# Result stores split over the batches: 128 KB stores with 32 batches outermost for 256 KB stores with four time quarters outermost

## Chip, cores and metric

One core of a Trainium2 chip runs the whole program. The metric is the device time of one execution in microseconds (us), lower is better. The core has a TensorE, a VectorE, a ScalarE, a GpSimd and a SyncE queue, and 16 DMA engines shared by all transfers.

## What is computed

`x` is 64 batches x 128 channels x 2048 times, fp32. First a mixing of channels by a matrix that each batch chooses, with a residual. Then a long convolution along time per channel (a state-space kernel of 64 complex modes and a direct term `D`), masked by a length per batch, again with a residual.

```
x = x + einsum('bct,bcd->bdt', x, weights[cond])            # mixing
dt = exp(log_dt); A = -exp(log_A_real) + 1j * A_imag; dtA = A * dt[:, None]
Ct = Cc * (exp(dtA) - 1.0) / A
K = 2.0 * einsum('hn,hnl->hl', Ct, exp(dtA[:, :, None] * arange(T))).real
y = causal_convolution(x, K) + x * D[:, None]               # by an FFT of 2T
out = x + y * (arange(T)[None, :] < length[:, None])[:, None, :]
```

## The kernel before

The mixed `x` goes through a scratch in device memory, `u_scratch`, laid out so that one channel and 32 batches are a tile of 128 rows of 512 times: row `t * 32 + b` holds quarter `t` of the time for batch `b` (`NBW` = 32, `UNIT` = 512 elements or 2 KB, `HALF` = 1024). The work after the mixing runs in 64 slots (`NSL`). A slot handles four such tiles, v = 0 to 3. A wide slot takes four channels and one half of the batches, the others two channels and both halves (`channel(s, v)`, `batches(s, v)`). The first 12 slots (`WIDE`) are wide, later every fourth one is. `made` slots compute the tables of their channels anew, the others load tables that were stored.

The engines run a software pipeline over `c`, the slot number, to `NSL + 2`. In turn `c` TensorE transposes the rows of slot c + 1 (`transpose_u`, L774), makes states of slot c (L797, L814) and the outputs of slot c - 1 (L835, L841, L853), in eight steps k. ScalarE empties output banks into `o_sb` (L972), VectorE then lays the unmasked input over it (`overlay`, L1255: where a batch is past its length the input stands in the result) and counts it in `s_ov`. In the first ten turns (`LATER` = 10) TensorE also mixes the last 28 batches (L752), two or three of them in a turn, in between these steps; their stores to `u_scratch` and the loads of `x_f` go with them.

`o_sb` is four buffers of 128 rows x 2 tiles x 512 elements. Buffer `2 * (s % 2) + v // 2` holds tiles 2p and 2p + 1 of slot s. ScalarE waits at L971 until the stores of the slot two before have landed (`s_store`). Nearly all transfers are issued by SyncE, in a fixed order. In a later turn `c` it is: the first half of `u_row` for slot c + 2 (`load_u`, L426), the table transposed by DMA (`transpose_g`, L486) or loaded (L472) for slot c + 1, the stores of tiles 2 and 3 of slot c - 2, the second half of `u_row`, the Toeplitz table (L440), at times a table of `g` (L462), and the stores of tiles 0 and 1 of slot c - 1. `load_u` waits for the overlay that frees its buffer:

```python
b, last = ROW_AT[s], before(ROW_AT, s)
if last is not None:
    sp.wait_ge(s_ov, 4 * last + 2 * p + 2)
```

In the turns with mixing, `mixing_slot`, the store of tile 3 of slot c - 2 is issued in step 0 and those of tiles 0, 1 and 2 of slot c - 1 in steps 3, 5 and 7, among stores to `u_scratch` (`store_half`, L417) and loads of `x_f` (L407). Two of the last slot's stores are issued by ScalarE.

Of the kernel before, what the change touches and what calls it, by code (L numbers as in the profile page):

```python
# [16 lines left out]
NB, H, T = 64, 128, 2048  # L17
# [16 lines left out]
UNIT = 512  # L34
# [9 lines left out]
NBW = NB // 2  # L44
# [3 lines left out]
LATER = len(MIXED)  # L48
# [17 lines left out]
NSL = len(SLOTS)  # L66
# [48 lines left out]
def before(places, i):  # L115

    last = [j for j in range(i) if places[j] == places[i]]
    return last[-1] if last else None
# [27 lines left out]
def build(nc, x, cond, length, w_in, log_dt, c_in, log_a, a_im, d_in, out):  # L146
# [8 lines left out]
    with ctx:  # L155
        def sb(name, shape, dt, where=ctx):
            return where.enter_context(nc.sbuf_tensor(name, shape, dt))

        def sem(name):
            return ctx.enter_context(nc.semaphore(name))  # L160
# [87 lines left out]
        o_sb = [sb(f"o_sb{i}", [P, 2, UNIT], F32, outs) for i in range(4)]  # L248
# [20 lines left out]
        s_store = [sem(f"s_store{i}") for i in range(4)]  # L269
# [9 lines left out]
        s_out, s_y, s_ov = (sem(n) for n in ("s_out", "s_y", "s_ov"))  # L279
# [17 lines left out]
        def has(c):  # L297
            return 0 <= c < NSL

        def wait(eng, s, value):  # L300
            if value > 0:
                eng.wait_ge(s, value)
# [31 lines left out]
        def mixing_over(eng):  # L334
            batch_mixed(eng, NB - 1)
# [11 lines left out]
        def channel(s, v):  # L347
            return SLOTS[s].first + (v if SLOTS[s].wide else v // 2)

        def batches(s, v):  # L350
            return SLOTS[s].part if SLOTS[s].wide else v % 2
# [35 lines left out]
                stored_g(eng, last)  # L387
            return gt_sb[GT_AT[unit.of]][:, unit.part, :, :, :].rearrange("p a b m -> p (a b m)"), half

        def store_out(eng, s, v):  # L390

            o = 2 * (s % 2) + v // 2
            eng.wait_ge(s_ov, 4 * s + v + 1)
            dst = bass.AP(out.tensor, batches(s, v) * NBW * H * T + channel(s, v) * T, [[UNIT, 4], [H * T, NBW], [1, UNIT]])
            eng.dma_start(dst, o_sb[o][:, v % 2, :]).then_inc(s_store[o], 16)  # L395

        @block.sync
        def _(sp):
# [4 lines left out]
            def load_x(n):  # L403
                last = before(X_AT, n)
                if last is not None:
                    batch_mixed(sp, last)
                sp.dma_start(x_f[X_AT[n]][:, :], x[n, :, :]).then_inc(s_x[X_AT[n]], 16)  # L407

            def store_half(n, j):
                if n < FIRST:  # L410
                    sp.wait_ge(s_ev, 2 * n + j + 1)
                else:
                    for q in (2 * j, 2 * j + 1):
                        evacuated(sp, UNIT_OF[Unit(True, n, q)])
                b = STAGE_AT[2 * n + j]
                dst = bass.AP(u_dram, (n // NBW * P + 2 * j * NBW + n % NBW) * UNIT, [[2 * TILE, H], [NBW * UNIT, 2], [1, UNIT]])
                sp.dma_start(dst, stage[b][:, :].rearrange("p (a t) -> p a t", t=UNIT)).then_inc(s_us[b], 16)  # L417

            def load_u(s, p):
# [4 lines that stand above are left out]
                step = (channel(s, 1) - channel(s, 0)) * 2 + batches(s, 1) - batches(s, 0)  # L424
                src = bass.AP(u_dram, (channel(s, 2 * p) * 2 + batches(s, 2 * p)) * TILE, [[UNIT, P], [step * TILE, 2], [1, UNIT]])
                sp.dma_start(u_row[b][:, HALF * p:HALF * (p + 1)].rearrange("p (v t) -> p v t", t=UNIT), src)\  # L426
                    .then_inc(s_row[b][p], 16)

            def load_toeplitz(s):
                t0, n = TABS[s][0], len(TABS[s])  # L430
                together = n == 2 and TOEP_AT[t0] % 4 < 3 and TOEP_AT[t0 + 1] == TOEP_AT[t0] + 1
                for t in [t0] if together else TABS[s]:
                    for r in range(t, t + 1 + together):
                        last = before(TOEP_AT, r)
                        if last is not None:
                            sp.wait_ge(s_out, 4 * (SLOT_OF[last] + 1))
                    b, rows_ = TOEP_AT[t], 4 * (1 + together)
                    src = bass.AP(k_dram, PAIR_OF[t] * (4 * KROW), [[1, P], [KROW, rows_], [1, Q]])
                    to = ap((toep_now, toep_later)[b // 4], b % 4 * 4 * Q, [[Q, rows_], [1, Q]])
                    sp.dma_start(to, src).then_inc(s_t[b], 16)  # L440

            def store_g(s):

                t = TABS[s][0]
                r = t // 2 % (GS // 2)
                sp.wait_ge(s_g, 4 * (MADE_NO[t] + 2))
                dst = bass.AP(g_dram, PAIR_OF[t] * P * 4 * Q, [[4 * Q, P], [P * 4 * Q, 2], [1, 4 * Q]])
                sp.dma_start(dst, ap(g_all, t % GS * 4 * Q, [[4 * Q, 2], [1, 4 * Q]])).then_inc(s_gst[r], 16)
                for unit in turns_of(s):
                    evacuated(sp, UNIT_OF[unit])  # L450
                dst = bass.AP(gt_dram, PAIR_OF[t] * P * 4 * Q, [[4 * Q, P], [P * 4 * Q, 2], [1, 4 * Q]])
                sp.dma_start(dst, ap(gt_now, 0, [[4 * Q, 2], [1, 4 * Q]])).then_inc(s_gtst[r], 16)
# [71 lines left out]
            def mixing_slot(c):  # L524
                for k in range(8):
                    if k == 0:
                        if c > 0:
                            load_toeplitz(c)
                        if has(c - 2):
                            store_out(sp, c - 2, 3)  # L530
                        load_u(c + 1, 1)
                    if k == 1:
                        store_g(c)
                    if k == 3 and c == 0:
                        sp.wait_ge(s_kd, 80)
                        load_toeplitz(c)
                    if k in (3, 5, 7) and has(c - 1):
                        store_out(sp, c - 1, k // 2 - 1)
                    if k == 5:
                        load_u(c + 2, 0)  # L540
                    for u in UNITS_AT[c][k]:
                        n, q = UNITS[u].of, UNITS[u].part
                        if UNITS[u].batch and q % 2 == 1:
                            store_half(n, q // 2)
                        if UNITS[u].batch and q == 3 and n + 3 < NB:
                            load_x(n + 3)

            def slot(c):
                if c < LATER:
                    mixing_slot(c)  # L550
                    return
                if c == LATER:
                    load_toeplitz(c)
                    store_out(sp, c - 2, 3)
                    load_u(c + 1, 1)
                    stages_landed(sp, range(STAGES // 2), NB)
                    mixing_over(sp)
                    load_toeplitz(c + 1)
                if has(c + 2):
                    load_u(c + 2, 0)  # L560
                if c < WIDE:
                    store_g(c)
                if c + 1 >= WIDE and has(c + 1):
                    if SLOTS[c + 1].made:
                        transpose_g(c + 1)
                    else:
                        load_gt(c + 1)
                if has(c - 2) and c > LATER and c - 2 < NSL - 1:
                    for v in (2, 3):
                        store_out(sp, c - 2, v)  # L570
                if has(c + 2):
                    load_u(c + 2, 1)
                    load_toeplitz(c + 2)
                    if not SLOTS[c + 2].made:
                        load_g(c + 2)
                if has(c - 1) and c - 1 < NSL - 1:
                    for v in range(2):
                        store_out(sp, c - 1, v)
                elif has(c - 1):
                    for v in (0, 2):  # L580
                        store_out(sp, c - 1, v)

            slots(slot)
            for o in range(4):
                sp.wait_ge(s_store[o], 32 * (NSL // 2))

        @block.gpsimd
        def _(pool):
# [304 lines left out]
        def _(act):  # L893
# [73 lines left out]
            def out_evac(s, v):  # L967
                o = 2 * (s % 2) + v // 2
                act.wait_ge(s_out, 4 * s + v + 1)
                if v % 2 == 0:  # L970
                    wait(act, s_store[o], 32 * (s // 2))  # L971
                act.activation(o_sb[o][:, v % 2, :], bank[:, 2 + v % 2, :], ACT.Copy, scale=1.0 / (US * KS))\  # L972
                    .then_inc(s_y, 1)

# [29 lines left out]
                                g_hi(t)  # L1004

            slots(slot)
            for v in (1, 3):
                store_out(act, NSL - 1, v)

        @block.vector  # L1010
        def _(dve):
# [302 lines left out]
```

## Time and profile before

| | |
|---|---|
| median of 3 runs | 1378.93 us (1374.29 to 1379.3) |
| profiled execution | 1383.85 us, span 1381.8 us |
| TensorE busy | 1099.5 us (80% of the span) |
| VectorE, ScalarE, GpSimd busy | 763.9, 576.3, 580.1 us |
| granted TensorE clock | 0.915 of full |
| moved by DMA | 330.88 MB, 239 GB/s over the span |
| stores of results | 254 issues on SyncE, 2 on ScalarE, 256 KB each |

In the rows, PE is TensorE and PEld its weight load, DVE VectorE, ACT ScalarE, POOL GpSimd, SPq and ACTq the queues from which SyncE and ScalarE issue transfers. L395 is line 395 of the kernel. PEclk is the granted clock as a share of 2.4 GHz, DMA share the mean busy share of the 16 DMA engines. Packets that overlap a little bring a share slightly over 1.

### The profile page before, as it was taken

What the parts mean: (1) busy time and instruction counts of PE and PEld (TensorE: products, weight loads), DVE (VectorE), ACT (ScalarE), POOL (GpSimd) and SP (SyncE); (2) the same over time, 40 slices, a digit from 0 to 9 for tenths busy, and PEclk for the clock granted to TensorE, in tenths of its full rate; (3) what the DMA queues carried; (4) which work ended last, traced back from release to release, by engine and by line L of the source; (5) the groups of instructions that cost most, each with busy time, mean ns of one, the idle gap of its engine ahead of it and who ended that gap; (6) DMA issues with size and microseconds to landing.
All of it is one profiled execution on the core that took longest, in us unless ns stands there. A gap on an engine that the chain in (4) does not pass through costs nothing.

```text
span 1381.8 us, 33160 instructions
## 1 busy us (share of the span) xinstructions
PE 1099.5 (80%) x12910; PEld 835.4 (60%) x12910; DVE 763.9 (55%) x1754; ACT 576.3 (42%) x1275; POOL 580.1 (42%) x1377
## 2 busy tenths in 40 slices
PE   8787858877877698787888787888778888888783
PEld 4332425555555467676767766767667767676663
DVE  5989314544544346556555565656555565656552
ACT  3544433333443334344444444444444444444431
POOL 2110388433433424453543444444644435444500
PEclk9999979988998889999999999999999998999987
DMA  9999999888988876997979897979988898979782
GB/s 349 408 416 416 415 351 346 305 295 293 314 317 296 282 243 194 177 191 193 184 196 175 193 163 186 190 195 197 167 205 172 203 171 195 193 192 195 161 145 101
DMA packets 218107, 330.88 MB, mean 239 GB/s; under 512 B 53138, under 2 KB 98578, under 8 KB 209762
## 3 DMA queue, kind: packets, MB, share of 16 engines
q1 hardware_dynamic: 217530, 328.05, 86.6%
q8 instruction: 104, 1.70, 0.6%
q0 software_dynamic: 160, 0.20, 0.1%
q10 hardware_dynamic: 264, 0.52, 0.1%
q14 instruction: 49, 0.40, 0.1%
HBM read 171.25 MB, written 147.00 MB: 230 GB/s over the span
## 4 chain that ended last, share of the span: by engine, by line
DMA 48%; PE 34%; SPq 7%; DVE 4%; ACT 3%; issue 3%; POOLq 0%; DVEq 0%; POOL 0%; ACTq 0%
DMA u_row<-u_scratch 36%; DMA u_scratch<-stage 9%; PE bank L835 6%; PE bank L853 6%; PE bank L752 6%; PE bank L774 5%; PE bank L797 4%; SPq L395 3%; PE bank L740 3%; PE bank L841 2%; PE bank L814 2%; SPq L462 2%; DVE o_sb L1255 2%; DVE u_t L1233 1%; ACT u_t L949 1%
## 5 line engine op out<-in xcount | busy, mean ns | idle before, releaser
L774 PE MATMUL bank<-ident,u_row 128*128 128x128 f32 x1024 | 295.6, 292 | 188.4 <-DMA u_row<-u_scratch 183.2
L853 PE MATMUL bank<-g_sb,st_sb 128*128 128x256 f16 x1536 | 330.0, 288 | 2.1 <-issue 2.1
L637 POOL TENSOR_TENSOR g_sb<-g_x,g_sb 128x128 f16<-128x128 f32 x256 | 103.0, 436 | 497.6 <-ACT g_sb L921 497.6
L1233 DVE SCALAR_TENSOR_TENSOR u_t<-bank,u_t 128x512 f16<-128x512 f32 x256 | 176.0, 688 | 192.1 <-ACT u_t L949 191.1
L774 PEld LDWEIGHTS bank<-ident,u_row 128*128 128x128 f32 x1024 | 150.5, 148 | 214.5 <-DMA u_row<-u_scratch 195.5
L965 ACT ACTIVATE st_sb<-bank 128x128 f16<-128x128 f32 x448 | 123.9, 277 | 309.3 <-PE bank L814 214.4
L949 ACT ACTIVATE u_t<-bank 128x512 f16<-128x512 f32 x256 | 151.9, 594 | 192.1 <-PE bank L774 192.1
L1238 DVE TENSOR_TENSOR st_sb<-bank,st_sb 128x128 f16<-128x128 f32 x448 | 130.2, 291 | 171.2 <-ACT st_sb L965 165.5
L835 PE MATMUL bank<-toep,u_t 128*128 128x192 f16 (+1 forms) x1752 | 208.4, 226 | 0.0
L1255 DVE COPY_PREDICATED o_sb<-mask,u_row 128x512 f32<-128x512 uint8 x256 | 194.5, 760 | 17.0 <-issue 16.9
L853 PEld LDWEIGHTS bank<-g_sb,st_sb 128*128 128x128 f16 x1536 | 156.9, 103 | 11.0 <-issue 2.4
L740 PE MATMUL bank<-x_f,w_buf 128*128 128x512 f32 x280 | 133.4, 626 | 36.0 <-issue 23.7
L835 PE MATMUL bank<-toep_later,u_t 128*128 128x192 f16 (+1 forms) x1320 | 156.7, 227 | 2.7 <-issue 2.7
L814 PE MATMUL bank<-st_sb,lam_sb 128*128 128x32 f16 (+1 forms) x3168 | 147.2, 184 | 10.1 <-issue 7.4
L972 ACT ACTIVATE o_sb<-bank 128x512 f32<-128x512 f32 x256 | 152.9, 598 | 4.4 <-DMA out<-o_sb 2.2
L814 PEld LDWEIGHTS bank<-st_sb,lam_sb 128*128 128x128 f16 x3168 | 132.3, 97 | 37.0 <-issue 21.8
L835 PEld LDWEIGHTS bank<-toep,u_t 128*128 128x128 f16 x1752 | 139.7, 103 | 11.0 <-issue 3.5
L629 POOL TENSOR_TENSOR g_x<-g_x,g_y 128x128 f32<-128x128 f32 x256 | 126.1, 523 | 5.0
L752 PE MATMUL bank<-x_f,w_buf 128*128 128x512 f32 x232 | 125.0, 648 | 2.3 <-ACT stage L926 1.9
L644 POOL TENSOR_TENSOR lam_sb<-eyes,lam_v 128x128 f16<-128x128 f16 x256 | 110.2, 459 | 32.3 <-PE bank L814 32.2
L740 PEld LDWEIGHTS bank<-x_f,w_buf 128*128 128x128 f32 x280 | 53.5, 199 | 110.6 <-issue 100.2
L936 ACT ACTIVATE stage<-bank 128x1024 f32<-128x1024 f32 x70 | 70.4, 1022 | 113.6 <-DMA u_scratch<-stage 74.6
(142 smaller groups left out, 1545.0 us busy)
## 6 DMA issues: line engine op xcount, KB each, us to landing
x_f<-in_x SPq DMA_DIRECT2D x64, 1024.0 KB, 14.1
u_scratch<-stage SPq DMA_DIRECT2D x128, 512.0 KB, 12.3
u_row<-u_scratch SPq DMA_DIRECT2D x128, 512.0 KB, 9.6
out<-o_sb SPq DMA_DIRECT2D x254, 256.0 KB
toep<-k_scratch SPq DMA_DIRECT2D x16, 512.0 KB, 10.9
g_scratch<-g_sb SPq DMA_DIRECT2D x12, 512.0 KB, 8.9
gt_scratch<-gt_sb SPq DMA_DIRECT2D x12, 512.0 KB, 8.9
toep_later<-k_scratch SPq DMA_DIRECT2D x24, 256.0 KB, 7.9
```

The costliest lines, as they stand in the source:

```text
L629: pool.tensor_tensor(out=g_x[r][:, h, part], in0=g_x[r][:, h, part], in1=g_y[:, h, part], op=SUB)\
L740: last = pe.matmul(bank[:, 4 * (n % 2) + k, :], w_buf[n % WS][:, :], x_f[X_AT[n]][:, k * 512:(k + 1) * 512], start=True, stop=True)
L752: last = pe.matmul(to, w_buf[of % WS][:, :], x_f[X_AT[of]][:, part * 512:(part + 1) * 512], start=True, stop=True)
L774: ins = pe.transpose(bank[:, u_bank(s, v), k % 4 * P:(k % 4 + 1) * P], ap(u_row[b], v * UNIT + g * Q + tb * P, [[1, P]]), ident[:, :])
L814: last = pe.matmul(ap(bank, v * 2 * P + at(j), [[2 * P, n], [1, NBW]]), lam_sb[t % LS][:, h, a, :, :].rearrange("p k m -> p (k m)"), st_sb ...
L835: pe.matmul(bank[:, y, col + tb * P + NM:col + Q], ap(u_t[s % 3], v * 2 * UNIT + a * UNIT + tb * 2 * P + gr * P, [[1, P]]), tp[:, h, b, NM ...
L853: last = pe.matmul(bank[:, y, col:col + Q], st_sb[s % 2][:, v, a, gr * P:(gr + 1) * P], g_sb[t % GS][:, h, b, :], start=False, stop=(m == ...
L949: act.activation(u_t[s % 3][:, q, 0, :], bank[:, u_bank(s, q), :], ACT.Copy, scale=US).then_inc(s_uh, 1)
L972: act.activation(o_sb[o][:, v % 2, :], bank[:, 2 + v % 2, :], ACT.Copy, scale=1.0 / (US * KS))\
L1233: dve.scalar_tensor_tensor(out=t[:, q, 1, :], in0=bank[:, u_bank(s, q), :], scalar=US, in1=t[:, q, 0, :], op0=MUL, op1=SUB).then_inc(s_ul, 1)
L1238: dve.tensor_tensor(out=state(s, 1, j), in0=new_state(j), in1=state(s, 0, j), op=SUB).then_inc(s_stl, 1)
L1255: dve.copy_predicated(o_sb[2 * (s % 2) + v // 2][:, v % 2, :].rearrange("p (b t) -> p b t", t=P), where.rearrange("p (b t) -> p b t", t=P) ...
```

## The change

`store_out` stores a pair of tiles (one `o_sb` buffer) with one issue for each quarter of the time, so that a transfer is 32 batches x 2 tiles x 2 KB. Eight issues of 128 KB take the place of four of 256 KB in each slot. Both overlays of the pair are waited for. In the turns with mixing the pair of tiles 0 and 1 is stored in step 5, behind `load_u`, and that of tiles 2 and 3 in step 0 of the next turn. The waits on `s_store` count 64 for 32.

```diff
-        def store_out(eng, s, v):
-
-            o = 2 * (s % 2) + v // 2
-            eng.wait_ge(s_ov, 4 * s + v + 1)
-            dst = bass.AP(out.tensor, batches(s, v) * NBW * H * T + channel(s, v) * T, [[UNIT, 4], [H * T, NBW], [1, UNIT]])
-            eng.dma_start(dst, o_sb[o][:, v % 2, :]).then_inc(s_store[o], 16)
+        def store_out(eng, s, p, times=range(4)):
+
+            o = 2 * (s % 2) + p
+            eng.wait_ge(s_ov, 4 * s + 2 * p + 2)
+
+            def place(v):
+                return (batches(s, v) * NBW * H + channel(s, v)) * T
+
+            for t in times:
+                dst = bass.AP(out.tensor, place(2 * p) + t * UNIT, [[H * T, NBW], [place(1) - place(0), 2], [1, UNIT]])
+                eng.dma_start(dst, o_sb[o][t * NBW:(t + 1) * NBW, :, :]).then_inc(s_store[o], 16)
...
                         if has(c - 2):
-                            store_out(sp, c - 2, 3)
+                            store_out(sp, c - 2, 1)
                         load_u(c + 1, 1)
...
-                    if k in (3, 5, 7) and has(c - 1):
-                        store_out(sp, c - 1, k // 2 - 1)
                     if k == 5:
                         load_u(c + 2, 0)
+                        if has(c - 1):
+                            store_out(sp, c - 1, 0)
...
-                    store_out(sp, c - 2, 3)
...
-                if has(c - 2) and c > LATER and c - 2 < NSL - 1:
-                    for v in (2, 3):
-                        store_out(sp, c - 2, v)
+                if has(c - 2):
+                    store_out(sp, c - 2, 1, range(2) if c - 2 == NSL - 1 else range(4))
...
-                if has(c - 1) and c - 1 < NSL - 1:
-                    for v in range(2):
-                        store_out(sp, c - 1, v)
-                elif has(c - 1):
-                    for v in (0, 2):
-                        store_out(sp, c - 1, v)
+                if has(c - 1):
+                    store_out(sp, c - 1, 0)
...
-                sp.wait_ge(s_store[o], 32 * (NSL // 2))
+                sp.wait_ge(s_store[o], 64 * (NSL // 2))
...
-                    wait(act, s_store[o], 32 * (s // 2))
+                    wait(act, s_store[o], 64 * (s // 2))
...
-            for v in (1, 3):
-                store_out(act, NSL - 1, v)
+            store_out(act, NSL - 1, 1, range(2, 4))
```

## Rows read from the trace of the kernel before

**Rows 1.** The page: busy engines; 40 equal slices in tenths and in GB/s.
```profile
PE 1099.5 (80%) x12910; PEld 835.4 (60%) x12910; DVE 763.9 (55%) x1754; ACT 576.3 (42%) x1275; POOL 580.1 (42%) x1377
...
PE   8787858877877698787888787888778888888783
...
DMA  9999999888988876997979897979988898979782
GB/s 349 408 416 416 415 351 346 305 295 293 314 317 296 282 243 194 177 191 193 184 196 175 193 163 186 190 195 197 167 205 172 203 171 195 193 192 195 161 145 101
```

**Rows 2.** Windows: length, busy of each engine, then PEclk, DMA share, GB/s.
```profile
50.00:230.00 180.00, 133.35 (x657) 61.88 (x655) 112.27 (x292) 73.25 (x94) 67.36 (x158) 0.93 1.01 392
240.00:534.00 294.00, 232.66 (x2479) 166.80 (x2477) 139.12 (x294) 112.03 (x252) 113.30 (x286) 0.87 0.85 291
534.00:1343.00 809.00, 666.67 (x9368) 566.05 (x9367) 467.58 (x1094) 358.18 (x886) 375.37 (x868) 0.93 0.88 184
1343.00:1355.20 12.20, 10.59 (x155) 7.59 (x151) 6.68 (x19) 4.69 (x14) 0.00 (x0) 1.00 0.42 98
1363.00:1380.00 17.00, 0.00 (x0) 0.00 (x0) 0.00 (x0) 0.00 (x0) 0.00 (x0) 0.55 0.26 102
```

**Rows 3.** Source line L1255, 534 to 1343 us: count, ns min/median/max, first and last start.
```profile
L1255 DVE COPY_PREDICATED o_sb<-mask,u_row x208: 724/734/1606, 535.2 to 1342.3; 128x512 f32<-128x512 uint8 x104
```

**Rows 4.** SyncE's timeline, 684 to 711 us: start, length, what.
```profile
684.12 1.69 SPq L395 DMA_DIRECT2D out<-o_sb  x2
...
688.35 3.16 SPq L395 DMA_DIRECT2D out<-o_sb  x2
691.56 1.20 SPq L426 DMA_DIRECT2D u_row<-u_scratch  x1
...
698.67 1.61 SPq L395 DMA_DIRECT2D out<-o_sb  x2
...
706.29 2.62 SPq L395 DMA_DIRECT2D out<-o_sb  x2
708.96 0.73 SPq L426 DMA_DIRECT2D u_row<-u_scratch  x1
...
710.24 0.50 SPq L472 DMA_DIRECT2D gt_later<-gt_scratch  x1
```

**Rows 5.** Overlays begun by 673.5 us; store issues begun by 684 us.
```profile
L1255 DVE COPY_PREDICATED o_sb<-mask,u_row x76: 726/733/1046, 240.2 to 673.3; 128x512 f32<-128x512 uint8 x76
...
L395 SPq DMA_DIRECT2D out<-o_sb x74: 537/570/6506, 245.1 to 675.3; - x74
```

**Rows 6.** Issues over the span, ns min/median/max; the landing line is that of L426.
```profile
L395 SPq DMA_DIRECT2D out<-o_sb x254: 537/732/6506, 245.1 to 1363.4; - x127
...
L426 SPq DMA_DIRECT2D u_row<-u_scratch x128: 360/1384/3317, 187.5 to 1327.7; - x128
...
DMA to landing us min/median/max: 4.9/9.6/16.2
...
L486 SPq DMA_TRANSPOSE gt_later<-g_sb x40: 1784/2922/3897, 569.3 to 1338.2; - x40
```

**Rows 7.** Timeline of the end.
```profile
1340.11 28.54 SPq L395 DMA_DIRECT2D out<-o_sb  x12
...
1345.75 2.44 PE L797 MATMUL bank<-u_t,gt_later 128*128 128x448 f16 x12 [1.59 <-DMA gt_later<-g_sb]
...
1360.90 0.60 ACT L972 ACTIVATE o_sb<-bank 128x512 f32<-128x512 f32 x1 [2.24 <-DMA out<-o_sb]
...
1362.17 0.73 DVE L1255 COPY_PREDICATED o_sb<-mask,u_row 128x512 f32<-128x512 uint8 x1
...
1362.93 0.55 ACTq L395 DMA_DIRECT2D out<-o_sb  x1
```

**Rows 8.** Waits: total us, times, longest; 240 to 534, then 534 to 1343 us.
```profile
PE bank L774 <- DMA u_row<-u_scratch: 58.7, 11, 9.0
...
PE bank L774 <- DMA u_row<-u_scratch: 117.7, 57, 5.2
```

**Rows 9.** The page: the chain that ended last, shares of the span by line.
```profile
DMA u_row<-u_scratch 36%; DMA u_scratch<-stage 9%; PE bank L835 6%; PE bank L853 6%; PE bank L752 6%; PE bank L774 5%; PE bank L797 4%; SPq L395 3%; PE bank L740 3%; PE bank L841 2%; PE bank L814 2%; SPq L462 2%; DVE o_sb L1255 2%; DVE u_t L1233 1%; ACT u_t L949 1%
```

## The prediction

> **What bounds the kernel now.** I read the page's top line and its slices first, then windows of five stretches, then the waits, then SyncE's own timeline. No compute engine is full: TensorE is busy 80% of the span, VectorE 55%, while the slices show the DMA engines busy nine tenths nearly everywhere [rows 1]. The odd thing is what they move: 408 to 416 GB/s in slices 2 to 4, but 145 to 205 GB/s from slice 16 on, at the same busy tenths. The windows say the same in numbers: 392 GB/s at a share of 1.01 before any result is stored, 184 GB/s at a share of 0.88 later [rows 2]. So "busy" there does not mean "moving".
>
> The last window explains it. From 1363 to 1380 us no compute engine runs and only result stores are in flight: the DMA share is 0.26 and the rate 102 GB/s. 0.26 of 16 engines is 4.2, so a store uses four engines, each at 102 / 4 = 25.5 GB/s. That is as much as one engine moves in the early stretch (392 / 16 = 24.5), so these four are at full speed; the other twelve do nothing for a store. One 256 KB store (0.262 MB) takes 0.262 MB / 102 GB/s = 2.57 us of those four, and the four stores of a slot 10.3 us.
>
> Now the load of these four in the long stage without mixing (534 to 1343 us). 208 overlays, one for each store, fall in it, so it is 52 slots of 809 / 52 = 15.6 us [rows 3]. It moves 184 GB/s x 809 us = 148.9 MB; 208 stores are 54.5 MB, so 94.4 MB is other traffic, spread over 16 engines: 94.4 MB / 392 GB/s = 241 us, 4.6 us a slot. Four engines thus have 10.3 + 4.6 = 14.9 us of work in a slot of 15.6 us. They are full, which is more than any compute engine is. In the mixing stage (240 to 534 us) the sum is 85.6 MB in all, 34 stores among them (256 in the kernel, less 208, less the 14 issued after 1340 us): 34 x 2.57 = 87 us and 76.7 MB / 392 GB/s = 196 us, 283 us of 294. They are full there too.
>
> The kernel feels it through SyncE and `u_row`. From 684 to 711 us SyncE goes from one issue to the next without a gap, and it is late: 76 overlays had begun by 673.3 us, while the 75th and 76th store are the first two issued after 684 us, ten us behind, with `u_row` loads between them in the same order [rows 4, 5]. The same store issue takes 0.54 us at best and 6.5 at worst [rows 6]. In the tail, where SyncE issues stores alone, 12 take 28.5 us, 2.4 us each, near the 2.57 us that four engines need to move one [rows 7]. So an issue takes as long as it takes to make room on those four. What is issued then waits behind them: a 512 KB load would move in 0.524 MB / 392 GB/s = 1.3 us and has landed in 4.9 us at best, but its median is 9.6 [rows 6]. TensorE stands before its transposes (L774) for these loads: 58.7 us in the mixing stage, 117.7 in the later one [rows 8], and 36% of the chain that ended last is `u_row<-u_scratch` [rows 9].
>
> **The change part by part.** (1) *Outermost dimension 32 for 4.* The bytes, the 2 KB pieces and their number stay (128 pieces for each old store, 2 x 64 in two of the eight new issues), and only their division over engines changes. The trace of before has no transfer with an outermost 32. The nearest rows are those with an outermost 128, which fill 16 engines (share 1.01 at 392 GB/s, half of it `u_scratch` stores in 2 KB pieces a constant 512 KB apart), and the store itself at 102 GB/s. So the 1.05 MB of a slot take 2.7 us of every engine at the one end, and 10.3 us of every engine at the other. I take the first: the new store is like the `u_scratch` store in piece size, direction and wide pitch. The four full engines then have 2.7 + 4.6 = 7.3 us a slot, and the mixing stage 85.6 MB / 392 = 218 us.
>
> The Trainium skill says how that division is made (DMA: Bandwidth & Descriptors, Queues, rings and completion order): a transfer runs on the largest number of engines up to 16 that divides the slowest dimension on both sides. By it, 4 and 128 give 4, as the tail window shows (0.26), and 32 and 32 give 16, which no row here shows. Another page speaks against the change (SBUF — State Buffer, Door 1: The DMA port swizzle): 32 adjacent partitions reach 8 of 16 ports, some 218 GB/s at most. An estimate by that page: 1.05 MB a slot at 218 GB/s is 4.8 us instead of 2.7, so 9.4 us a slot and about 237 us for the mixing stage, still less than TensorE wants in either. No row here shows a store from 32 partitions on all engines.
>
> (2) *What TensorE gets back, later stage.* With the four engines at half load, the 117.7 us of waits on `u_row` go; with SyncE on time, a load goes out more than half a slot before it is wanted. Work also runs at half clock now and then: granted 0.93 is 14% of 809 us, 113 us at 1.2 GHz, 57 us lost. The clock falls after such pauses; I count 20 of the 57. Together 138 us, or 12.9 us a slot. A check from a stretch with no load in the way: 1343 to 1355.2 us is a slot of 12.2 us at clock 1.00, with 1.6 us of it waiting for a transposed table [rows 2, 7]. Below 12.2 it will hardly go. Bounds: 70 us (six tenths of the waits) to 170 us (all waits and nearly all clock).
>
> (3) *Mixing stage.* 58.7 us of waits on `u_row`; TensorE's own need is then 235 us, the DMA engines' 218. Both are close to full and will not interlock perfectly, and here the load is issued only after the second overlay of the slot before, some three of eight steps ahead of its use. I take 255 us, a gain of 39; bounds 15 and 60.
>
> (4) *The tail.* SyncE issues its last 14 stores from 1340 us on, 28.5 us for twelve of them; ScalarE's copy at 1360.90 us waited 2.24 us for one of them to land, the last overlay starts at 1362.17, the last issue at 1362.93, and the span ends at 1381.8 [rows 7]. These 19 us are backlog: at most 14 x 2.57 = 36 us after 1340. Without it, one 128 KB store lands a few us after its issue (nearest: 4.9 us, the fastest `u_row` landing), so 16 us go, bounds 10 and 18 (the 2.24 us included).
>
> (5) *Eight issues for four.* An issue costs SyncE 0.54 us when nothing blocks it, so four more are 2.2 us a slot, on a queue whose other records shrink: `u_row` from a median of 1.4 us towards the 0.73 in [rows 4], the stores from 1.1 on average there to 0.54. A slot with two transposing loads then has 8 x 0.54 + 2 x 0.73 + 2 x 2.9 + 0.5 = 12.1 us [rows 4, 6], below 12.9. I cost it at nothing, under cover of TensorE; without that cover see the second rival. ScalarE's two issues stay two.
>
> (6) *Stores by pairs.* `store_out` now waits for both overlays of a pair. In the later stage SyncE next issues `load_u`, which waits on that same second overlay, so nothing behind it is later than before. In the mixing stage `load_u(c + 2, 0)` comes ahead of the store, two stores move to the next slot's start, and `load_u(c + 1, 1)` has four issues ahead of it for one; but that one took up to 6.5 us where it met full queues [rows 6], and four free ones take 2.2. `o_sb` has over a slot of slack before ScalarE wants it (L971), and at the tail, where it waited for it [rows 7], the stores land sooner. I cost this part at nothing.
>
> **Sum.** The profiled execution took 1383.85 us, its span 1381.8. 1383.85 - 138 - 39 - 16 = 1190.9. The median of the runs lies 4.9 us below the profiled one, so 1186. Bounds from the parts: 1379 - 70 - 15 - 10 = 1284, and 1379 - 170 - 60 - 18 = 1131.
>
> **The rivals.**
> *Loads still late* (13 in 100). Only half of the waits were due to the backlog; the rest comes from transposing loads, which now hold their engines long too, or from the order of SyncE's issues. For: `gt_later` loads are waited for as well [rows 7]. Against: the best landing is half the median. Gain 59 + 15 + 14: about 1290.
> *SyncE becomes the bound, slower than before* (6 in 100). If an issue's length is its own and not a matter of room, then from 684.12 to 710.74 us (26.6 us) eight stores took 9.1 us and the rest 17.5 [rows 4]. Sixteen at 0.75 us, the median, make 12 + 17.5 = 29.5, 11% more; over 809 us that is 89 us, less some 35 from mixing and tail: about 1433. It decides above (26.6 - 17.5) / 16 = 0.57 us an issue. Against: 0.54 us where the queues are empty, and the 2.4 us of the tail, where issue and drain agree.
> *The store doesn't speed up* (5 in 100). If pieces written 1 MB apart by 16 engines at once, from 32 partitions, go at the present 102 GB/s, all 16 engines have the 14.9 us that four have now: about 1375, no change. For: no row of this shape. Against: the 512 KB pitch at 392 GB/s. At 200 GB/s it would cost nothing yet (5.2 + 4.6 us a slot). [...]
> *The first case*, as summed: 72 in 100, its own range 1135 to 1260; 4 in 100 left for what I don't see, spread as the rest.
>
> **Numbers.** Measurement tells a change from none at about 0.5%, 7 us. Faster: the first case and the late loads, 0.72 + 0.13 and most of the 4, gives 0.89; same 0.06; slower 0.05 (the SyncE case, a little trimmed, as its break-even lies above the free issue). The range takes the first two cases: 1131 to 1287.
>
> **What would show it.** Right: DMA share and rate in the tail window no longer at 0.26, GB/s above 210 and DMA share below 0.75 in the later stage, `u_row` landing at 5 to 7 us median, L774's waits near zero, slots near 13 us, the end within 7 us of the last overlay, SyncE idle between issues. Wrong: store issues of 0.6 us and more back to back (rival two); a DMA share of 0.9 with a low rate (rival three); `u_row` landing soon but issued late (rival one).

## The result, and the profile after

The changed kernel takes 1112.4 us (median of 4 runs, 1110.4 to 1114.9) for 1377.3: a ratio of 0.808, 95% interval 0.805 to 0.811. That is 19% less time, and below the range on record (1131 to 1287). The direction and the mechanism were forecast, the size was not: 191 us were expected to go, 265 went.

The page of the kernel after, its busy engines and its slices, answers to [rows 1]:

```profile
PE 1021.2 (92%) x12910; PEld 793.0 (72%) x12910; DVE 768.2 (69%) x1754; ACT 573.6 (52%) x1275; POOL 635.0 (57%) x1377
...
PE   8877784889898999899999999999999999999998
...
PEclk9999997889999999999999999999999999999999
DMA  9999999899999999989999999999999999899994
GB/s 342 415 408 416 418 414 389 295 361 362 394 372 386 372 388 341 327 211 292 208 261 255 260 264 220 260 226 258 280 229 255 239 254 280 206 263 217 267 215 125
```

TensorE is busy nine tenths or more in all slices from 18 to 39, and its clock stays up from slice 10 on. The DMA busy share alone hides the difference: it is at least as high as before, while by the windows below 24% more is moved a second in the mixing stage and 33% more in the later one.

The stages can be compared exactly. 208 overlays (L1253 is the L1255 of before) and 831 recorded transposes of each kind fall between 476.6 and 1086.8 us here, as many as between 534 and 1343 us before. Windows of the kernel after, against [rows 2]:

```profile
240.00:476.60 236.60, 219.48 (x2485) 159.59 (x2483) 141.66 (x294) 111.92 (x252) 125.11 (x289) 0.96 1.01 362
476.60:1086.80 610.20, 602.61 (x9363) 530.53 (x9360) 469.47 (x1093) 355.19 (x885) 419.18 (x868) 1.00 0.97 245
1086.80:1108.40 21.60, 16.51 (x254) 13.22 (x250) 10.85 (x30) 7.74 (x19) 0.00 (x0) 0.95 0.48 130
...
L1253 DVE COPY_PREDICATED o_sb<-mask,u_row x208: 727/742/1021, 477.6 to 1086.2; 128x512 f32<-128x512 uint8 x104
```

| stage | before | after | gain | forecast |
|---|---|---|---|---|
| mixing, from 240 us | 294.0 | 236.6 | 57.4 | 39 |
| later, 52 slots | 809.0 | 610.2 | 198.8 | 138 |
| tail | 38.8 | 21.6 | 17.2 | 16 |

The sum, 273.4 us, is the difference of the spans. The later stage is where the miss lies. There TensorE's idle time went from 809 - 666.7 = 142.3 us to 610.2 - 602.6 = 7.6, and its busy time from 666.7 to 602.6 for the same work: 134.7 and 64.1 us. A slot takes 610.2 / 52 = 11.7 us.

Issues of the kernel after (nanoseconds min/median/max), and then the time to landing of L431, which is L426 of before; it answers to [rows 6]:

```profile
L400 SPq DMA_DIRECT2D out<-o_sb x510: 315/432/3087, 251.5 to 1105.1; - x170
...
L431 SPq DMA_DIRECT2D u_row<-u_scratch x128: 359/437/1853, 185.1 to 1070.1; - x128
...
DMA to landing us min/median/max: 4.2/5.6/17.1
```

A `u_row` load lands in 5.6 us for 9.6, and its issue takes 0.44 us for 1.38. The waits of the kernel after against [rows 8]: in the mixing stage

```profile
PE bank L773 <- DMA u_row<-u_scratch: 14.2, 8, 3.4
```

remains of 58.7 us, and in the later stage nothing of 117.7.

### The profile page after: what moved, and what is told of

Its sections match the earlier page's. It is cut to its first block, busy times and chain, and to the rows that moved or that the text cites. A ratio compares the mean times of both kernels' runs of the same rounds, so it can differ in the third digit from the quotient of the medians.

```text
span 1108.4 us, 33416 instructions
## 1 busy us (share of the span) xinstructions
PE 1021.2 (92%) x12910; PEld 793.0 (72%) x12910; DVE 768.2 (69%) x1754; ACT 573.6 (52%) x1275; POOL 635.0 (57%) x1377
## 4 chain that ended last, share of the span: by engine, by line
PE 74%; DMA 19%; ACT 2%; issue 2%; SPq 2%; DVE 1%; DVEq 0%; ACTq 0%
PE bank L834 15%; PE bank L852 14%; PE bank L796 12%; DMA u_scratch<-stage 10%; PE bank L773 10%; PE bank L813 7%; PE bank L751 7%; DMA u_row<-u_scratch 6%; PE bank L840 5%; PE bank L739 3%; DMA gt_scratch<-gt_sb 2%; ACT stage L935 1%; DMA x_f<-in_x 1%; SPq L400 1%; DVE o_sb L1253 0%
## 5 line engine op out<-in xcount | busy, mean ns | idle before, releaser
L852 PE MATMUL bank<-g_sb,st_sb 128*128 128x256 f16 x1536 | 308.4, 274 | 0.3 <-issue 0.3
L773 PE MATMUL bank<-ident,u_row 128*128 128x128 f32 x1024 | 279.1, 276 | 19.4 <-DMA u_row<-u_scratch 18.3
L636 POOL TENSOR_TENSOR g_sb<-g_x,g_sb 128x128 f16<-128x128 f32 x256 | 115.9, 487 | 265.1 <-ACT g_sb L920 265.1
L1253 DVE COPY_PREDICATED o_sb<-mask,u_row 128x512 f32<-128x512 uint8 x256 | 199.1, 778 | 16.2 <-issue 16.0
L834 PE MATMUL bank<-toep,u_t 128*128 128x192 f16 (+1 forms) x1752 | 198.0, 221 | 1.8 <-issue 1.8
L773 PEld LDWEIGHTS bank<-ident,u_row 128*128 128x128 f32 x1024 | 144.7, 142 | 31.3 <-DMA u_row<-u_scratch 20.8
L739 PE MATMUL bank<-x_f,w_buf 128*128 128x512 f32 x280 | 130.7, 616 | 35.9 <-issue 24.5
L852 PEld LDWEIGHTS bank<-g_sb,st_sb 128*128 128x128 f16 x1536 | 150.0, 98 | 6.7 <-issue 0.6
L834 PE MATMUL bank<-toep_later,u_t 128*128 128x192 f16 (+1 forms) x1320 | 145.5, 219 | 0.7 <-issue 0.7
L834 PEld LDWEIGHTS bank<-toep,u_t 128*128 128x128 f16 x1752 | 133.0, 99 | 10.4 <-issue 4.5
L628 POOL TENSOR_TENSOR g_x<-g_x,g_y 128x128 f32<-128x128 f32 x256 | 132.9, 550 | 5.0
L751 PE MATMUL bank<-x_f,w_buf 128*128 128x512 f32 x232 | 119.7, 624 | 3.8 <-ACT stage L925 3.5
```

The source lines that it names most:

```text
L628: pool.tensor_tensor(out=g_x[r][:, h, part], in0=g_x[r][:, h, part], in1=g_y[:, h, part], op=SUB)\
L739: last = pe.matmul(bank[:, 4 * (n % 2) + k, :], w_buf[n % WS][:, :], x_f[X_AT[n]][:, k * 512:(k + 1) * 512], start=True, stop=True)
L751: last = pe.matmul(to, w_buf[of % WS][:, :], x_f[X_AT[of]][:, part * 512:(part + 1) * 512], start=True, stop=True)
L773: ins = pe.transpose(bank[:, u_bank(s, v), k % 4 * P:(k % 4 + 1) * P], ap(u_row[b], v * UNIT + g * Q + tb * P, [[1, P]]), ident[:, :])
L834: pe.matmul(bank[:, y, col + tb * P + NM:col + Q], ap(u_t[s % 3], v * 2 * UNIT + a * UNIT + tb * 2 * P + gr * P, [[1, P]]), tp[:, h, b, NM ...
L852: last = pe.matmul(bank[:, y, col:col + Q], st_sb[s % 2][:, v, a, gr * P:(gr + 1) * P], g_sb[t % GS][:, h, b, :], start=False, stop=(m == ...
```

## The experiments

Ratios are to the kernel before on the same chip, with 95% intervals. Windows "of equal work" hold the same 208 overlays as those above. The changed kernel itself was run once more, beside the next experiments:

> The changed kernel as it is, as the measure for its neighbours on this chip: 1110 to 1128 us, given that two kernels with its very instructions took 1120 and 1125.

1109.8 us, ratio 0.807 (0.804 to 0.810). 

**Two runs that tested nothing.** The store's outermost dimension was to be 4 (4 x 8, as here) and 8 (8 x 4) for 32:

```diff
-                dst = bass.AP(out.tensor, place(2 * p) + t * UNIT, [[H * T, NBW], [place(1) - place(0), 2], [1, UNIT]])
+                dst = bass.AP(out.tensor, place(2 * p) + t * UNIT, [[8 * H * T, 4], [H * T, 8], [place(1) - place(0), 2], [1, UNIT]])
```

> Only the outermost dimension of the eight new stores is undone: 4 x 8 batches for 32; issues, bytes, order and pairs stay. Theory A (a store runs on as many engines as its outermost dimension allows, and the four full engines were the bound): four engines again have 10.3 us of stores and 4.6 us of other traffic in a slot, so about 1370 us, a share of 0.26 in the tail, full SyncE. Rival B (the gain came from the shape of the issues, the pairs and the order): within 1% of the changed kernel, 1112 us. If both count, between.

> The same with 8 x 4 batches. Theory A: eight engines at 25.5 GB/s, 204 GB/s, so the stores of a slot take 5.1 us of these eight, 9.7 us with the rest, less than TensorE's 11.4; in the mixing stage 196 + 44 = 240 us of 245. So no loss in the later stage, a few us in the mixing one: 1112 to 1135 us. If the gain were proportional to the engines, it would lie half way, near 1245. Rival B: 1112.

1124.7 us (0.814, 0.807 to 0.821) and 1120.2 us (0.812, 0.806 to 0.818). The issues in both traces have 32 rows of two pieces, as in the changed kernel: neighbouring dimensions that make one even step were merged. They are of use in another way: two more copies of the same instructions lie 8 to 15 us above the two runs of the changed kernel. So a difference of up to 15 us between runs on different chips says nothing here.

**The number of engines alone.** So the kernel before was taken, with a shape that can't be merged. Its rows land at other places of the result than they belong:

```diff
-            dst = bass.AP(out.tensor, batches(s, v) * NBW * H * T + channel(s, v) * T, [[UNIT, 4], [H * T, NBW], [1, UNIT]])
+            i = (SLOTS[s].first - H1) // 2
+            if SLOTS[s].wide:
+                batch, first = SLOTS[s].part * NBW + 8 * v, SLOTS[s].first
+            else:
+                batch, first = i % 2 * NBW + 8 * v, H1 + i // 2 * 4
+            dst = bass.AP(out.tensor, (batch * H + first) * T, [[UNIT, 16], [H * T, 8], [1, UNIT]])
```

> The two runs with 4 x 8 and 8 x 4 batches tested nothing: the dimensions were merged back into 32 when the kernel was built. So the question is put to the kernel before instead. Here it keeps its four issues of 256 KB a slot, their 128 source partitions, their 2 KB pieces with a pitch of 1 MB inside, their places in SyncE's order and their waits; only the outermost dimension on the side of the result is 16 (16 x 8 for 4 x 32), which puts the rows at other places of the result. Theory A (the number of engines is the cause): 16 engines, 2.7 us of each in a slot, SyncE with half the issues of the changed kernel: 1095 to 1125 us. Rival B (pairs, quarters and order carry it): 1350 to 1380 us.

1106.8 us, ratio 0.805 (0.801 to 0.810). The whole gain, with four issues a slot, at the old places in SyncE's order. Theory A holds and rival B falls. With 8 x 16:

> The same with 8 x 16. Theory A: eight engines at 25.5 GB/s have 5.1 us of stores and 4.6 of other traffic in a slot, below TensorE's 11.4, and 240 us in the mixing stage: 1110 to 1150 us, far nearer to the changed kernel than to the middle (1245). Rival B: 1350 to 1380.

1132.3 us, ratio 0.825 (0.822 to 0.829). As theory A says, eight engines are nearly enough. That these really are 4, 8 and 16 engines can be counted in the pages. The two stores issued by ScalarE have a queue to themselves, here in the kernel before, with 8 x 16, with 16 x 8, and in the changed kernel (packets, MB, share):

```profile
q10 hardware_dynamic: 264, 0.52, 0.1%
...
q10 hardware_dynamic: 272, 0.52, 0.1%
...
q10 hardware_dynamic: 288, 0.52, 0.1%
...
q10 hardware_dynamic: 160, 0.26, 0.1%
```

Two stores of 128 pieces are 256 packets, and 8, 16 and 32 are left over: 4, 8 and 16 for each store. Two stores of 64 pieces in the changed kernel are 128, and again 16 are left for each. The two runs that tested nothing have 160 too. Windows of equal work of the run with 16, mixing stage and later stage, and then of the run with 8:

```profile
240.00:479.90 239.90, 217.58 (x2454) 158.27 (x2453) 140.18 (x289) 111.77 (x251) 123.31 (x288) 0.95 1.00 356
479.90:1082.90 603.00, 601.39 (x9362) 530.98 (x9358) 468.38 (x1093) 354.62 (x885) 420.86 (x868) 1.00 0.92 248
```
```profile
240.00:489.90 249.90, 218.15 (x2437) 158.28 (x2435) 139.69 (x289) 111.07 (x250) 118.04 (x282) 0.95 0.95 338
489.90:1104.70 614.80, 604.93 (x9364) 532.24 (x9361) 469.52 (x1093) 355.10 (x885) 417.99 (x868) 1.00 1.00 243
```

With eight engines the mixing stage takes 10 us more, at 338 GB/s for 356, and the later stage 12 us more, 8 of them idle time of TensorE. These are most of the 25 us between the two medians.

The store issues of the run with 16, against [rows 6]:

```profile
L400 SPq DMA_DIRECT2D out<-o_sb x254: 538/562/2372, 242.3 to 1099.3; - x127
```

The issue has the same size and place as before. Its median went from 0.73 to 0.56 us and its longest from 6.5 to 2.4 us, so the long issues of the kernel before belong to its four full engines.

**The other part alone.** Pairs and order of the changed kernel, tiles stored in the old form:

```diff
-            for t in times:
-                dst = bass.AP(out.tensor, place(2 * p) + t * UNIT, [[H * T, NBW], [place(1) - place(0), 2], [1, UNIT]])
-                eng.dma_start(dst, o_sb[o][t * NBW:(t + 1) * NBW, :, :]).then_inc(s_store[o], 16)
+            for j in range(2) if len(times) == 4 else [times[0] // 2]:
+                dst = bass.AP(out.tensor, place(2 * p + j), [[UNIT, 4], [H * T, NBW], [1, UNIT]])
+                eng.dma_start(dst, o_sb[o][:, j, :]).then_inc(s_store[o], 32)
```

> The other part of the change alone: pairs, places in the order and waits of the changed kernel, but each tile stored as before, 256 KB with the four quarters outermost, two issues for each pair. Theory A (the engines): nothing is gained, 1360 to 1385 us, a share of 0.26 in the tail. Rival B (the order carries part of it): below 1330.

1385.3 us, ratio 1.008 (1.004 to 1.012): nothing gained, 5 to 16 us lost by the interval. Its later stage and its tail, where only stores are in flight:

```profile
534.00:1340.00 806.00, 663.97 (x9389) 567.36 (x9387) 470.06 (x1099) 359.63 (x889) 378.94 (x868) 0.93 0.88 185
...
1357.00:1372.00 15.00, 0.00 (x0) 0.00 (x0) 0.11 (x1) 0.00 (x0) 0.00 (x0) 0.58 0.26 102
```

The same 0.88 and 0.93, the same 0.26 and 102 GB/s as in [rows 2].

**How many issues.** Quarters without pairs, first at the old places of the stores:

```diff
-            dst = bass.AP(out.tensor, batches(s, v) * NBW * H * T + channel(s, v) * T, [[UNIT, 4], [H * T, NBW], [1, UNIT]])
-            eng.dma_start(dst, o_sb[o][:, v % 2, :]).then_inc(s_store[o], 16)
+            for t in range(4):
+                dst = bass.AP(out.tensor, batches(s, v) * NBW * H * T + channel(s, v) * T + t * UNIT, [[H * T, NBW], [1, UNIT]])
+                eng.dma_start(dst, o_sb[o][t * NBW:(t + 1) * NBW, v % 2, :]).then_inc(s_store[o], 16)
```

> The kernel before with each 256 KB store split into four quarters of 64 KB with 32 batches outermost, at its old place: no pairs, no change of order, 16 issues a slot. Theory A: the gain is there without the pairs; SyncE has 16 x 0.4 = 6.4 us of store issues and 4.5 us of other issues in a slot of 11.4 us, just covered: 1115 to 1150 us. Rival B (pairs and order carry it): above 1250. Rival C (an issue has its own fixed length of 0.75 us): 16 x 0.75 + 4.5 = 16.5 us a slot, above 1350.

1216.4 us, ratio 0.881 (0.873 to 0.889), between the theories: the engines give it most of the gain, and something takes about 105 us of it away. Then at the new places (the counts of `s_store` doubled):

```diff
             for t in times:
-                dst = bass.AP(out.tensor, place(2 * p) + t * UNIT, [[H * T, NBW], [place(1) - place(0), 2], [1, UNIT]])
-                eng.dma_start(dst, o_sb[o][t * NBW:(t + 1) * NBW, :, :]).then_inc(s_store[o], 16)
+                for j in range(2):
+                    dst = bass.AP(out.tensor, place(2 * p + j) + t * UNIT, [[H * T, NBW], [1, UNIT]])
+                    eng.dma_start(dst, o_sb[o][t * NBW:(t + 1) * NBW, j, :]).then_inc(s_store[o], 16)
```

> The changed kernel with one tile an issue: 16 issues of 64 KB a slot, 32 batches outermost. The split of the old stores at their old places took 1216 us, its SyncE without a gap in the later stage. Theory H (that loss is SyncE's time for 16 issues, 0.5 us each): the same here, 1190 to 1225 us, the stores being all that differs from the changed kernel. Rival I (it was the old places of the stores): near 1115.

1217.0 us, ratio 0.884 (0.881 to 0.887), the same. SyncE's timeline in it, and then TensorE's wait for `u_row` from 534 to 1180 us (L774 there):

```profile
804.01 4.12 SPq L401 DMA_DIRECT2D out<-o_sb  x8
808.17 0.52 SPq L432 DMA_DIRECT2D u_row<-u_scratch  x1
808.73 0.49 SPq L446 DMA_DIRECT2D toep_later<-k_scratch  x1
809.27 4.22 SPq L401 DMA_DIRECT2D out<-o_sb  x8
813.53 0.44 SPq L432 DMA_DIRECT2D u_row<-u_scratch  x1
```
```profile
PE bank L774 <- DMA u_row<-u_scratch: 70.6, 36, 4.4
```

Eight stores take 4.1 to 4.2 us and hardly any time lies between the issues: now SyncE is the bound by its own time, 0.5 us an issue, and TensorE waits for `u_row` again. Theory H holds. It is rival two of the prediction at 16 issues. At eight it is not: four issues a slot (1107 us) and eight (1110 us) give the same time.

**What the stores still cost.** Only the first quarter of the result is stored:

```diff
-            for t in times:
+            for t in times[:1]:
```

> The changed kernel with only the first of the four quarters of the time stored (the first two of the last pair), so a quarter of the result traffic and two issues a slot. Theory D (in the later stage TensorE is the bound, in the mixing stage the DMA engines are): the later stage stays at 603 us within 8, the mixing stage loses up to 20 us of 245, the tail 1 to 2: 1088 to 1105 us. Rival E (the stores still hold everything up, as the DMA share of 0.98 suggests): below 1070.

1096.2 us, ratio 0.795 (0.789 to 0.801). Its mixing and later stage, windows of equal work:

```profile
240.00:470.40 230.40, 214.44 (x2453) 155.89 (x2452) 140.31 (x290) 111.44 (x251) 125.72 (x291) 0.97 0.96 343
470.40:1070.90 600.50, 600.50 (x9365) 530.73 (x9362) 466.53 (x1093) 354.51 (x885) 421.40 (x868) 1.00 0.75 180
```

Three quarters of the stores are worth 14 to 16 us against the two runs of the changed kernel, and 24 to 28 us against its two copies above, which ran on the same chip as this one. Against the windows of the changed kernel the mixing stage is 6 us shorter (230.4 for 236.6) and the later one 10 (600.5 for 610.2). In the later stage TensorE is busy all of the 600.5 us, at a clock of 1.00; with all stores it is busy 602.6 of 610.2. The stage is nearly TensorE's alone with or without them. Theory D holds, its 8 us for the later stage a little too narrow, and rival E falls.

**The clock.** The waits put back into the changed kernel, in a short and a long form (the second waits for `+ 4`, and only `if c > WIDE`):

```diff
                 if has(c + 2):
+                    sp.wait_ge(s_out, 4 * (c - 1) + 3)
                     load_u(c + 2, 0)
```

> The changed kernel, but in the later turns the first half of u_row is issued only when the third output of the slot before is ready (SyncE waits for it), so it lands about when or after TensorE wants it. Theory F (the pauses for u_row pull the clock down, and both cost): with 1.5 to 4 us of pause a slot, TensorE waits 75 to 200 us in the later stage and its granted clock there falls from 1.00 to 0.95 or less: 1210 to 1330 us, the sum of the waits and some 0.3 to 0.5 of them again in clock. Rival G (the clock fell in the kernel before for another reason): the clock stays at 0.99 or more and the loss is the waits alone.

> As the run with the late half of u_row, but SyncE waits for the fourth output of the slot before and only from turn 13 on, so that TensorE stands once a slot for 4 to 6 us instead of about 1.2 twice. The shorter pauses left the granted clock at 0.98. Theory F (long pauses pull the clock down, as in the kernel before, where they reached 5 us): the clock falls to 0.93 or less in the later stage, 51 x 5 = 255 us of waits and 40 us or more of clock: 1380 to 1450 us. Rival G (clock and pauses have nothing to do with each other): 0.98 and 1360 us.

1228.7 us (0.895, 0.892 to 0.899) and 1386.9 us (1.006, 1.004 to 1.009). The later stage in windows of equal work, and the wait for `u_row`, in the first and then in the second:

```profile
478.80:1199.70 720.90, 628.54 (x9363) 539.73 (x9360) 471.26 (x1093) 358.54 (x885) 392.22 (x868) 0.98 0.78 208
PE bank L774 <- DMA u_row<-u_scratch: 78.5, 64, 2.9
```
```profile
482.20:1363.40 881.20, 691.05 (x9365) 585.76 (x9362) 463.70 (x1093) 358.36 (x885) 358.10 (x868) 0.90 0.63 170
PE bank L775 <- DMA u_row<-u_scratch: 190.1, 50, 5.6
```

The same work keeps TensorE busy 602.6 us at clock 1.00 (the changed kernel), 628.5 at 0.98 and 691.0 at 0.90. In the first run the pauses average 78.5 / 64 = 1.2 us. TensorE is idle 92 us and busy 26 us longer; the clock accounts for 0.02 x 721 = 14 of these, and the rest was not traced. In the second the pauses average 3.8 us. TensorE is idle 190 us and busy 88 us longer, which is the clock's 0.10 x 881 = 88. So the long pauses cost nearly half of themselves again, the short ones a quarter, and a sixth by the clock alone. My expectation for the first (a clock of 0.95 or less) was wrong, its time was in the range. For the second the clock and the time came about as theory F says, with fewer waits (190 us for 255). The kernel before stands between: 142 us idle, 64 us busier, 0.07 x 809 = 57 of them by the clock. Rival G falls.

That the length of a pause counts, and not only their sum, is seen in the run with 16 issues at the old places. Its later stage and wait:

```profile
490.70:1184.90 694.20, 630.11 (x9364) 548.12 (x9360) 467.03 (x1092) 356.09 (x885) 398.06 (x868) 0.96 0.82 214
PE bank L775 <- DMA u_row<-u_scratch: 62.6, 30, 4.2
```

It is idle for only 64 us, less than the 92 of the short form, but in pauses of 2.1 us on average, and its clock is 0.96 for 0.98. One pause of the long form, with the stretches around it:

```profile
668.00:671.30 3.30, 3.30 (x62) 2.98 (x59) 2.61 (x8) 1.59 (x6) 0.00 (x0) 1.00 0.20 73
671.30:675.00 3.70, 0.04 (x2) 0.02 (x2) 1.93 (x5) 1.87 (x4) 1.73 (x5) 1.00 0.69 224
675.10:678.40 3.30, 3.30 (x28) 2.85 (x29) 0.00 (x0) 0.00 (x0) 3.22 (x10) 0.50 0.86 279
```

TensorE is fully busy at 2.4 GHz, stands, and finds itself at 1.2 GHz (0.50) when it goes on. In the later stage of the long form the granted clock fell 47 times in 49 pauses, in the short form 6 times in some 60.

**The order of the quarters.**

```diff
-            for t in times:
+            for t in sorted(times, key=lambda t: (t % 2, t)):
```

> The changed kernel with the quarters stored in the order 0, 2, 1, 3, so that consecutive issues read from partitions 0 to 31, 64 to 95, 32 to 63, 96 to 127. In the last stretch the new stores move at some 265 GB/s while active (98 GB/s at a share of 0.37), less than 392. If neighbours in the queue overlap and it is a matter of which partitions they read, the mixing stage, whose DMA share is 0.99, gains 2 to 8 us of 1110; if not, nothing: within 3 us.

1123.2 us, ratio 0.817 (0.814 to 0.821). No gain; the 13 us more are as much as copies of the same kernel differ. It moved 104 GB/s at a share of 0.39 in the last stretch, 267 GB/s while active, as without it.

**The rate of a store on 16 engines.** It was priced at 392 GB/s. In a stretch where stores are the only transfers, the changed kernel shows less:

```profile
1088.00:1100.00 12.00, 11.96 (x180) 9.16 (x178) 7.58 (x22) 4.90 (x13) 0.00 (x0) 1.00 0.37 98
```

98 / 0.37 = 265 GB/s: the rate while the engines are active. In the 16 x 8 run, with 128 source partitions, it is 169 / 0.62 = 273:

```profile
1095.00:1102.00 7.00, 4.45 (x76) 3.98 (x72) 2.94 (x8) 2.19 (x4) 0.00 (x0) 1.00 0.62 169
```

What both have is a pitch of 1 MB. The last run has rows 8 KB apart, in one issue for each tile, at places of the result where they don't belong:

```diff
-            for t in times:
-                dst = bass.AP(out.tensor, place(2 * p) + t * UNIT, [[H * T, NBW], [place(1) - place(0), 2], [1, UNIT]])
-                eng.dma_start(dst, o_sb[o][t * NBW:(t + 1) * NBW, :, :]).then_inc(s_store[o], 16)
+            for j in (range(2) if len(times) == 4 else range(times[0] // 2, times[0] // 2 + 1)):
+                dst = bass.AP(out.tensor, s * H * T + (2 * p + j) * UNIT, [[T, P], [1, UNIT]])
+                eng.dma_start(dst, o_sb[o][:, j, :]).then_inc(s_store[o], 32)
```

> The changed kernel with each tile stored in one issue of 256 KB from 128 partitions, its rows at a pitch of 8 KB (128 channels of one batch outermost) in place of 1 MB, at other places of the result. New stores moved at 265 GB/s while active from 32 partitions and the 16 x 8 form at 273 GB/s (169 at a share of 0.62) from 128 partitions, both with a pitch of 1 MB between engines' rows or batches, against 392 with four engines. Theory J (the wide pitch slows 16 engines writing at once): 350 GB/s and more while active in the last stretch, a DMA share below 0.90 in the later stage, and the mixing stage shorter by up to 10 us: 1090 to 1108 us. Theory K (16 engines storing at once go at about 270 whatever the place): 260 to 285 GB/s, DMA share as before, 1105 to 1120 us.

1104.9 us, ratio 0.800 (0.796 to 0.804). Its stretch with stores alone:

```profile
1080.00:1092.00 12.00, 11.96 (x184) 9.13 (x180) 8.04 (x22) 5.83 (x16) 0.00 (x0) 1.00 0.32 116
```

116 / 0.32 = 363 GB/s. Theory J is right about the rate, and wrong about the mixing stage (still a share of 0.99, and no shorter) and the later share (0.95). In time it is 5 to 8 us, not clear of the spread between copies. Number of issues and source partitions change with the pitch here, but the 16 x 8 run had both at the 1 MB pitch, and 273 GB/s.

## Why the prediction came out wrong

*What bounds the kernel* was right, and is shown: the outermost dimension alone, 16 for 4 in the kernel before, gives the whole gain, and the rest of the change alone gives none. One of its rows proves less than it was taken for. The twelve stores in 28.5 us of [rows 7] were read as issues that wait for room, but with 16 engines the same twelve take nearly as long, while the shortest issue there is 0.54 us:

```profile
1073.13 26.74 SPq L400 DMA_DIRECT2D out<-o_sb  x12
```

The stores of the tail follow the overlays. That issues wait for room is shown by their lengths, 0.73 us in the median and 6.5 at most for 0.56 and 2.4.

*Part 1, the price of a store on 16 engines*, 2.7 us a slot: 1.05 MB at 265 GB/s are 4.0. That it costs nothing up to 5.2 was said in the third rival, and it did not.

The Trainium skill's page on the ports (SBUF — State Buffer, Door 1: The DMA port swizzle) has 218 GB/s as the most that 32 partitions reach. Measured while active are 265 from 32 and 273 from 128 partitions, so their number made little difference here. Several stores from different partitions are in flight at once in these stretches, so no run tests a single one. The estimate by that page for the mixing stage, 237 us, was called less than TensorE wants, but TensorE's own need was put at 235 in part 3. The Trainium skill's table of measured facts (DMA: Bandwidth & Descriptors, Latency and other measured facts) has copies within device memory at 207 GB/s each way with a row pitch of 512 KiB, 164 with 2 MiB and 103 with 4 MiB, and nothing at 1 MiB. The direction agrees with the runs: with 16 engines a pitch of 1 MB cost a quarter to a third of the rate. The Trainium skill's rule for the number of engines (DMA: Bandwidth & Descriptors, Why a DMA increments its semaphore by 16 and not by 1) is the largest number up to 16 that divides the slowest dimension of both sides. It agrees with the packets counted above, and with the times on one chip: 4 in front 1374 us, 8 in front 1132, 16 in front 1107, 32 in front 1110.

*Part 2, the later stage, is the step that failed*: "I count 20 of the 57" and "below 12.2 it will hardly go". All 57 us of clock came back, for the granted clock there is 1.00. The 118 us of waits went as said, and with them 17 us of idle time of other names, which had no term. The busy time fell by 7 us beyond the clock's 57, which was not traced further. That is 199 us for 138, beyond even my bound of 170. The clock's term was too small by 37 us, more than the other two together. The runs with the waits put back show why the clock belongs to the waits: with pauses of 3.8 us it falls to 0.90. The floor was a misreading of a row that I had: the 12.2 us of [rows 2] held 1.6 us of waiting, named in the same sentence and not taken out. I took a stretch with a wait in it for the least a slot can take. It was no average slot either, with 155 matmuls for 9368 / 52 = 180. A slot now takes 11.7 us on average.

*Part 3, mixing*, 57 us for 39, within its bounds: waits fell from 58.7 to 14.2 us, and the granted clock rose from 0.87 to 0.96. All idle time of TensorE fell by 44 us, its busy time by 13. Part 3 had no term for the clock, and its "own need" of 235 us held the slow clock; and the allowance for "will not interlock perfectly" was too large.

*Part 4, the tail*, 17 for 16. *Part 5, eight issues*: right, though closer to the edge than the text shows; SyncE is bound at 16 (1217 us). Transposing issues were priced at 2.9 us each and took 1.27 in the median once the queues were emptier, and the others grew shorter too. *Part 6, pairs*: priced at nothing; alone they cost 5 to 16 us by the interval, and beside 16 engines no cost is seen (1107 us in the old order, 1110 in the new).

## What to carry to other kernels

Look at the share and the rate of the DMA engines together, in a stretch where one kind of transfer is alone: a share of 4/16 at full rate per engine meant here that the shape of the access pattern, not the memory, set the limit, and that the other transfers on those engines and the issuing queue waited behind it. When pauses of TensorE go, count their clock too: here up to 0.46 us for each us of long pauses. Read the floor of a stage from its busy time at full clock, over a stretch that holds as much work as the average. Trade issue count against engine count with the issuing queue's own cost in view: 0.5 us each, harmless at 8 a slot of 11.7 us, binding at 16.

## What the runs showed that I had not expected

Sixteen engines storing rows 1 MB apart move 265 to 273 GB/s, rows 8 KB apart 363, four engines at the 1 MB pitch 102 / 0.26 = 392 by the same reckoning. The DMA busy share stays at 0.97 in the later stage though TensorE waits for no load there, and falls only to 0.75 with a quarter of the stores: it isn't a measure of room. And short pauses (1.2 us on average, 64 of them) left the clock at 0.98, while 50 pauses of 3.8 us brought it to 0.90.
